# Taking the second router's logits from the weights: `Ws` beside the gate weights, `wo @ Ws` beside `wo`, no transposes of the normalised rows

## The chip, the core and the metric

The kernel runs on one core of a Trainium2 chip. The time is the device time of one execution in microseconds. Five engines matter: TensorE (PE, with its weight loads shown as PEld), VectorE (DVE), ScalarE (ACT), GpSimd (POOL) and SyncE (SP, which here only issues transfers).

## The reference: what is computed

One transformer-like layer on x of shape (8, 512, 256): 4,096 rows of 256, in 32 tiles of 128 rows (four to a batch).

```python
x = x + attention(layernorm(x), ...)      # mixture of 4 memories, gated linear attention,
                                          # ends in: o * rsqrt(mean(o*o)+eps) * norm_w * silu(x@w_g), then @ w_o
x = x + ffn(layernorm(x), Ws, bs, W1, b1, W2, b2)

def ffn(x, ...):                          # N = 4096 rows, E = 8 experts, k = N / E = 512
    route_prob = softmax(xf @ Ws + bs).T
    route_vals, routes = top_k(route_prob, k)
    xin = xf[routes]
    h = gelu(einsum('ekd,edf->ekf', xin, W1) + b1)
    out = (einsum('ekf,efd->ekd', h, W2) + b2) * route_vals
    # added back to the rows that were picked
```

The logits that matter here are `layernorm(x1) @ Ws + bs`, eight numbers a row, where x1 = x + attention output is the residual. A layer norm is (x1 - mean) * rstd, so the same logits are ((x1 @ Ws) - mean * colsum(Ws)) * rstd + bs. And x1 @ Ws is x @ Ws plus (normalised gated rows) @ (w_o @ Ws).

## The kernel before

All instructions are placed by hand on the engines' queues; semaphores order them. The program goes through five stages.

1. **Stage A (0 to 53 us).** For each batch b of 512 rows: DVE takes mean and variance of x and normalises it (`stats_a`, `norm_a`), POOL makes the reciprocal root, PE transposes the normalised rows (`a_transpose`, L1771), ACT copies them out as `xT` (L700), and PE multiplies them by `wgg`, which holds the gate weights w_g (256 columns) and the four columns of the first router, w_gate (`a_product`, L1786, 260 columns, 16 matmul records a batch since each f32 matmul shows as two). ACT makes `gs` (Silu) and `lg` of the result. In the same stage PE turns the low-rank gate weights (`low_rank_t`, before the product of batch 5) and multiplies them out (`merged_gate`, before that of batch 6); ACT copies both (L713, L722), and the next product waits for the first copy. SP issues the loads of x and of the weights and the zero fills of the scatter rooms (`clear_rooms`), one behind the other.
2. **The slots (53 to 463 us).** 24 slots, one attention group of 512 rows each. In slot s PE does, in this order: values, gate of s+1, `outputs(s-1)`, keys, queries, then the items of the output projection, keys turned, values, rows of s+2 turned, `scores(s)`, `updates(s)`. From slot 12 on the output projection and second norm of batch b are spread over the slots: `turned(b)` in slot 12+2b (PE transposes, L1990), `project(b)` in slot 13+2b (@ wo, 256 columns, 16 records), `residual(b)` right behind on DVE (L1271), row statistics on DVE in slot 14+2b (L1279, L1282) with the reciprocal root on ACT, `norm2(b)` on ACT in slot 15+2b (L824, four tiles of rows to `xn2`), `norm_t(b)` on PE in the same slot (eight transposes, L2014) with two ACT copies (L835), and `route(b)` in slot 16+2b (8 narrow matmuls against `wsb` = Ws, 16 records, attn<-wsb), whose result DVE takes to `l8` with the bias added (`router`, L1291). The items sit between fixed PE items of the slot; `scores(s)` waits for them since they share PSUM banks 0 to 3 (`attn`).
3. **The tail (443 to 487 us).** Batches 5, 6 and 7 come out behind the last slot. `outputs(22)` in slot 23 gives the last stored group; SP stores it, POOL gathers batch 7's eight pieces (L467), DVE combines them in two halves (L1302, L1307), then squares, head norm, gate, transposes, projection, residual (`residual_half`, L1333), statistics and second norm in halves, `norm_t_half`, `route_half`, the last logits, a softmax over the eight experts (L1457 to L1467), and the probabilities `p8` are turned on PE.
4. **The search (487 to 533 us).** 15 rounds of DVE, ACT (Sign, L956, after a table load L952) and PE find the 512 best rows of each expert; then the row lists are built.
5. **The experts (533 to 760 us).** Gathers, two products with W1 and W2 for eight experts, scatter with add.

Three orders around the change. SP's queue in the tail is `load_xr(6)`, `store_out(5)`, `store_xp(5)`, `load_xr(7)`, then the stores of 6 and 7. `store_xp(b)` (L642) waits for `norm2(b)`. The residual rows of batches b and b-2 share one buffer, so `load_xr(b)` (L632) waits until `norm2(b-2)` has read it:

```python
if b >= 2:
    sp.wait_ge(out_st[b % 2], 16 * (b // 2))
    sp.wait_ge(f_xn2, TB * (b - 1))
```

ACT's queue behind the last slot begins with `norm2(5)`. And behind the softmax it copies `b1c` (L950) and loads the table for Gelu and Sign (L952) while DVE finishes `p8`.

## Time and profile before

| | us |
|---|---|
| median of 3 runs | 802.74 |
| lowest and highest run | 800.09, 805.4 |
| span of the profiled execution, first to last instruction | 760.2 |
| PE busy | 695.7 (92% of the span) |
| PEld busy | 618.6 (81%) |
| DVE busy | 501.5 (66%) |
| ACT busy | 348.2 (46%) |
| POOL busy | 247.4 (33%) |

The profile gives the profiled execution by its span; the runs' time also holds what lies before the first and behind the last instruction, 42.5 us if the median is set against that span. Times in the trace are microseconds from the start of the span. The chain of work is followed back from the last instruction, at each step to what released it.

### The profile page before, as it was taken

The page shows a single profiled execution, that of the slowest core. Times are in us where ns is not written, and L with a number is a line of the kernel's source. Part 1 is how long each engine was busy: PE and PEld are TensorE (multiplying, and loading weights), DVE is VectorE, ACT ScalarE, POOL GpSimd, SP SyncE. Part 2 cuts the span into 40 slices and gives each one's busy share as a digit, 9 for nine tenths or more (in the row PEclk, how much of TensorE's full clock was granted, in tenths as well). Part 3 has the DMA queues.
Part 4 walks back from the last instruction along what each step waited for, and adds up shares of the span by engine and source line. Part 5 has one row for each costly group of instructions (what it writes and reads, how often), then busy time and mean ns, then how long its engine had stood idle before and what let it go on. Part 6 is the DMA issues. An engine that isn't in the chain of part 4 may idle for free.

```text
span 760.2 us, 25608 instructions
## 1 busy us (share of the span) xinstructions
PE 695.7 (92%) x11058; PEld 618.6 (81%) x11058; DVE 501.5 (66%) x1159; ACT 348.2 (46%) x765; POOL 247.4 (33%) x358
## 2 busy tenths in 40 slices
PE   7998998999989999999999999508999999999993
PEld 6886787989978999899899888407689998999992
DVE  6716774555446678777767677678378878877820
ACT  2663544445544546655656564530353345325410
POOL 5510044555644413223140431001734253203333
PEclk9998999999999999999999998755899999999997
DMA  7960024343443635454544453720735255312213
GB/s 201 391 276 2 31 99 153 109 135 124 157 149 112 196 96 158 135 165 140 168 109 142 138 164 108 262 49 3 233 130 154 54 156 139 120 21 28 29 21 36
DMA packets 75467, 96.81 MB, mean 127 GB/s; under 512 B 11337, under 2 KB 67057, under 8 KB 74202
## 3 DMA queue, kind: packets, MB, share of 16 engines
q1 hardware_dynamic: 62250, 69.52, 28.0%
q0 software_dynamic: 12288, 25.12, 13.2%
q8 instruction: 87, 1.43, 0.8%
q10 hardware_dynamic: 816, 0.53, 0.2%
q14 instruction: 26, 0.21, 0.1%
HBM read 53.78 MB, written 41.55 MB: 125 GB/s over the span
## 4 chain that ended last, share of the span: by engine, by line
PE 78%; DVE 10%; issue 4%; DMA 3%; POOL 2%; ACT 1%; POOLq 0%; DVEq 0%
PE bank L1828 41%; PE attn L1828 27%; PE bank L1786 3%; PE bank L1880 2%; DVE arena L1488 2%; PE bank L1887 1%; DMA arena<-x_p,idxs 1%; PE attn L2189 1%; DMA big<-o_m,gidx 1%; DVE st L1043 1%; PE attn L1771 1%; PE attn L1990 1%; POOL arena L524 1%; POOL big L467 1%; DVE big L1056 1%
## 5 line engine op out<-in xcount | busy, mean ns | idle before, releaser
L1828 PE MATMUL attn<-arena 32*32 32x64 f32 (+4 forms) x6048 | 140.3, 225 | 9.2 <-issue 7.3
L1828 PE MATMUL bank<-xT,arena 128*128 128x128 f32 (+2 forms) x964 | 145.8, 306 | 0.0
L1828 PEld LDWEIGHTS attn<-arena 32*32 32x32 f32 (+3 forms) x6048 | 114.2, 120 | 33.2 <-issue 15.4
L1828 PEld LDWEIGHTS bank<-xT,arena 128*128 128x128 f32 x964 | 124.3, 192 | 11.2 <-issue 5.8
L467 POOL DMA_INDIRECT big<-o_m,gidx x64 | 71.0, 1109 | 159.7 <-PE bank L1828 116.9
L460 POOL DMA_INDIRECT x_c<-big,sidx x64 | 68.6, 1071 | 119.3 <-PE bank L1828 88.9
L1828 PE MATMUL bank<-arena,xT 128*128 128x128 f32 (+2 forms) x640 | 107.1, 320 | 0.1
L1828 PEld LDWEIGHTS bank<-arena,xT 128*128 128x128 f32 x640 | 90.0, 199 | 8.6 <-issue 2.9
L543 POOL DMA_INDIRECT out_dram<-arena,idxs x32 | 50.2, 1569 | 109.6 <-ACT arena L1010 99.3
L1165 DVE COPY_PREDICATED arena<-causal,attn 128x1024 f32<-128x1024 int32 x24 | 31.6, 1316 | 71.2 <-PE attn L1828 71.2
L524 POOL DMA_INDIRECT arena<-x_p,idxs x32 | 34.3, 1070 | 98.8 <-DVE idxs L1567 70.8
L751 ACT ACTIVATE arena<-bank 128x512 f32<-128x512 f32 x48 | 28.7, 599 | 72.1 <-PE bank L1828 72.1
L1828 PE MATMUL bank<-zeros,arena 128*128 128x128 f32 x336 | 39.8, 275 | 0.0
L980 ACT ACTIVATE rmask<-attn 128x512 f32<-128x512 f32 x14 | 8.4, 597 | 67.8 <-PE attn L1828 67.4
L1828 PEld LDWEIGHTS bank<-zeros,arena 128*128 128x128 f32 x336 | 38.7, 192 | 0.1
L965 ACT ACTIVATE big<-big,b1c 128x256 f32<-128x256 f32 x84 | 37.3, 502 | 0.0
L758 ACT ACTIVATE arena<-arena 128x512 f32<-128x512 f32 x24 | 15.2, 633 | 41.9 <-DVE arena L1156 30.3
L1186 DVE SCALAR_TENSOR_TENSOR arena<-arena,bank 128x64 f32<-128x64 f32 x112 | 31.5, 282 | 4.0
L1786 PE MATMUL bank<-wgg,xT 128*128 128x260 f32 x128 | 29.6, 384 | 1.9 <-issue 1.5
L1199 DVE TENSOR_TENSOR_SCAN arena<-rmask,arena 128x512 f32<-128x512 f32 x24 | 29.4, 1226 | 0.8
L1786 PEld LDWEIGHTS bank<-wgg,xT 128*128 128x128 f32 x128 | 23.7, 190 | 5.6 <-issue 2.3
L772 ACT ACTIVATE arena<-attn 64x512 f32<-64x512 f32 x46 | 27.6, 601 | 0.6
(305 smaller groups left out, 1249.2 us busy)
## 6 DMA issues: line engine op xcount, KB each, us to landing
x_c<-zeros SPq DMA_DIRECT2D x8, 1024.0 KB, 9.2
xT<-x_c SPq DMA_DIRECT2D x16, 512.0 KB, 4.1
o_m<-arena SPq DMA_DIRECT2D x16, 512.0 KB, 4.0
xT<-in_L_ffn_W_dram SPq DMA_DIRECT2D x8, 1024.0 KB, 7.9
gs<-in_L_ffn_W_dram SPq DMA_DIRECT2D x8, 1024.0 KB, 7.6
xT<-in_L_attn_x_dram SPq DMA_DIRECT2D x8, 512.0 KB, 5.2
out_dram<-xT SPq DMA_DIRECT2D x8, 512.0 KB, 5.2
arena<-in_L_attn_x_dram SPq DMA_DIRECT2D x7, 512.0 KB, 6.2
```

Source lines behind the costliest of these rows:

```text
L460: nc.gpsimd.indirect_dma_start(x_c[b], bass.IndirectOffsetOnAxis(sidx[:, k, t:t + 1], 0), xn[:, t, :], None, bounds_check=MROWS - 1, oob_i ...
L467: nc.gpsimd.indirect_dma_start(og[:, b % 2, k, j, :], None, o_m[b], bass.IndirectOffsetOnAxis(gidx[:, k, t:t + 1], 0), bounds_check=MROWS ...
L524: nc.gpsimd.indirect_dma_start(xe[:, e % 3, j, :], None, x_p, bass.IndirectOffsetOnAxis(idxs[:, e, j:j + 1], 0), bounds_check=B * S - 1, o ...
L543: nc.gpsimd.indirect_dma_start(outf, bass.IndirectOffsetOnAxis(idxs[:, e, j:j + 1], 0), ye[:, e % 2, j, :], None, bounds_check=B * S - 1, ...
L751: nc.scalar.activation(vv[:, g % 2, 2 * h:2 * h + 2, :], bank[7].rearrange("p (j d) -> p j d", j=2), ACT.Copy).then_inc(d_vs, 1)
L772: ins = nc.scalar.activation(rows[CH * c:CH * c + CH, 2:4, :, :], heads[half(c, 2), 2:4, :, :], ACT.Copy)
L965: nc.scalar.activation(ht[:, f // FT % 2, f % FT, at], ht[:, f // FT % 2, f % FT, at], ACT.Gelu_apprx_tanh, bias=b1c[:, f:f + 1]).then_inc ...
L1165: nc.vector.copy_predicated(am[:, :, :, :], causal[:, :].bitcast(I32).unsqueeze(1).unsqueeze(1).to_broadcast([P, NH, TB, CH]), attn[:, :, ...
L1186: chained(nc.vector.scalar_tensor_tensor(vst[:, c, :], vst[:, c - 1, :], fe[:, g % 2, c - 1:c], u, ALU.mult, ALU.add))
L1199: nc.vector.tensor_tensor_scan(cum[:, :], rmask[:, :], ybuf[:, :], 0.0, ALU.mult, ALU.add)\
L1786: ins = nc.tensor.matmul(bank[4 + j][:, 0:D + M], xT[:, b, k, P * j:P * j + P], wgg[:, k, :], start=(k == 0), stop=(k == 1))
L1828: return nc.tensor.matmul(out_, l, r, start=a, stop=z, skip_group_check=True)
```

## The change

Ws becomes eight more columns of `wgg`, so `a_product` gives x_norm @ Ws beside the gate (268 columns), and `lg` grows to 12 columns. `wo` is scaled by norm_w already in stage A (its two loads move ahead of most weight loads on SP; the scaling moves from slot 7), turned by four more PE transposes in `low_rank_t`, copied by ACT (`wot`), and multiplied by Ws in `merged_gate` (four matmuls, and two more against ones that give the column sums of Ws), so that `wo` has eight more columns, wo @ Ws. Two small ACT copies take these out. POOL turns x_norm @ Ws back to x @ Ws for all rows (`xs`, four operations behind stage A). `project` writes 264 columns into four banks instead of 256 into half banks; `residual` adds `xs` and the eight columns into `l8` with one more DVE operation. `norm_t` and `route`, their ACT copies and the DVE operation `router` are gone, in the slots and in the tail. In their place DVE finishes the logits by four dependent operations (`centred`, `logits`): once for 24 tiles at the end of slot 23, once for batch 6, once for each half of batch 7. The statistics of all batches are kept. In the tail `norm2(5)` moves on ACT from the start of the queue to behind the head norm of batch 7's halves; `norm2_half(1)` moves behind the exponentials, and its shift on DVE behind `p8`; 56 and 24 dummy matmuls (`warm`) stand where 32 and 8 stood.

```diff
-        flat = [ctx.enter_context(nc.psum_tensor(f"bank{i}", [P, 512], F32)) for i in range(4, 8)]
-        bank = [attn[:, i, :] for i in range(4)] + [t[:, :] for t in flat]
+        upper_banks = ctx.enter_context(nc.psum_tensor("bank", [P, 4, 512], F32))
+        bank = [attn[:, i, :] for i in range(4)] + [upper_banks[:, i, :] for i in range(4)]
...
-        wgg = sb("wgg", [P, 2, D + M])
-        wo = sb("wo", [P, 2, D])
+        wgg = sb("wgg", [P, 2, D + M + E])
+        wo = sb("wo", [P, 2, D + E])
...
+            pool.wait_ge(a_lg, NT)
+            pool.wait_ge(w_z, W_Z)
+            nc.gpsimd.tensor_tensor(stda[:, :], vare[:, :, :].rearrange("p b j -> p (b j)"),
+                                    rstda[:, :, :].rearrange("p b j -> p (b j)"), ALU.mult).then_inc(x_s, 1)
+            nc.gpsimd.tensor_tensor(xs_m[:, :, :], means.to_broadcast([P, NT, E]),
+                                    negsum[:, :].unsqueeze(1).to_broadcast([P, NT, E]), ALU.mult).then_inc(x_s, 1)
+            pool.wait_ge(x_s, 1)
+            nc.gpsimd.tensor_tensor(xs[:, :, :], lg[:, :, M:M + E], over_experts(stda[:, :]), ALU.mult).then_inc(x_s, 1)
+            pool.wait_ge(x_s, 3)
+            nc.gpsimd.tensor_tensor(xs[:, :, :], xs[:, :, :], xs_m[:, :, :], ALU.subtract).then_inc(x_s, 1)
...
+            sp.dma_start(wo[:, :, 0:D], kp(w_o)).then_inc(wo_in, 16)
+            for h in range(2):
+                sp.dma_start(nwc[HDV * h:HDV * h + HDV, :], norm_w.rearrange("(n a) -> n a", a=1)).then_inc(wo_in, 16)
...
             clear_rooms(4, B)
-            sp.dma_start(wo[:, :, :], kp(w_o)).then_inc(w_in2, 16)
-            for h in range(2):
-                sp.dma_start(nwc[HDV * h:HDV * h + HDV, :], norm_w.rearrange("(n a) -> n a", a=1)).then_inc(w_in2, 16)
-            sp.dma_start(wsb[:, :, :], kp(Ws)).then_inc(w_in2, 16)
...
+            act.dma_start(wgg[:, :, D + M:D + M + E], kp(Ws)).then_inc(wg_in, 16)
...
+                nc.scalar.activation(wot[:, :, :], upper_banks[:, 2:4, D:2 * D], ACT.Copy)
...
-            norm2(LAST - 2)
             out_t(LAST - 1, (4, 7))
             group_out_last()
             squares_half(0)
-            norm_t(LAST - 2)
             squares_half(1)
             head_rstd_half(0)
             head_rstd_half(1)
+            norm2(LAST - 2)
             out_t_half(0)
             out_t_half(1)
             row_rstd(LAST - 1)
             norm2(LAST - 1)
             row_rstd_half(0)
             norm2_half(0)
-            norm_t(LAST - 1)
             row_rstd_half(1)
-            norm2_half(1)
-            norm_t_half(0)
-            norm_t_half(1)
             for k, (lo, hi) in enumerate(PARTS):
                 act.wait_ge(s_sub, k + 1)
                 nc.scalar.activation(pr[:, lo:hi, :], l8[:, lo:hi, :], ACT.Exp).then_inc(s_exp, 1)
-
+            norm2_half(1)
 
             act.wait_ge(b1_t, 1)
...
+            dve.wait_ge(wo_in, 16 * 3)
+            nc.vector.tensor_scalar(wo[:, :, 0:D], wo[:, :, 0:D], nwc[:, 0:1], None, ALU.mult).then_inc(wo_n, 1)
...
+                nc.vector.tensor_tensor(l8[:, t, :], rows[:, :, D:D + E], xs[:, t, :], ALU.add).then_inc(f_l, 1)
 
...
-            def router(b):
-                dve.wait_ge(f_l, b + 1)
...
+            def lstep(ins):
+                l8_done[0] += 1
+                ins.then_inc(f_l8, 1)
+                dve.wait_ge(f_l8, l8_done[0])
...
+            def centred(lo, hi, from_):
+                n, at = hi - lo, slice(lo, hi)
+                dve.wait_ge(f_mv, hi)
+                dve.wait_ge(f_l, from_)
+                lstep(nc.vector.tensor_tensor(lm[:, at, :], mv[:, at, 0:1].to_broadcast([P, n, E]),
+                                              negsum[:, :].unsqueeze(1).to_broadcast([P, n, E]), ALU.mult))
+                lstep(nc.vector.tensor_tensor(l8[:, at, :], l8[:, at, :], lm[:, at, :], ALU.add))
+
+            def logits(lo, hi, from_):
+                n, at = hi - lo, slice(lo, hi)
+                dve.wait_ge(f_rstd, from_)
+                lstep(nc.vector.tensor_tensor(l8[:, at, :], l8[:, at, :],
+                                              rstd[:, at].unsqueeze(2).to_broadcast([P, n, E]), ALU.mult))
+                lstep(nc.vector.tensor_tensor(l8[:, at, :], l8[:, at, :],
+                                              bsb[:, :].unsqueeze(1).to_broadcast([P, n, E]), ALU.add))
 
...
-                    router(logit)
                 if stats is not None:
                     row_stats(stats)
                 if s == NG - 1:
                     row_stats(LAST - 2)
                     head_scaled(LAST - 1)
                     norm_shift(LAST - 2)
+                if s == NG - 1:
+                    dve.wait_ge(w_in2, 16 * W_IN2)
+                    centred(0, TB * (LAST - 1), LAST - 1)
+                    logits(0, TB * (LAST - 1), LAST - 1)
                 if s >= 1:
                     masked(s)
 
             gated(LAST - 1)
-            router(LAST - 3)
             states(NG - 1)
             combine_half(0)
             combine_half(1)
...
+            centred(TB * (LAST - 1), TB * LAST, LAST)
             norm_shift(LAST - 1)
+            logits(TB * (LAST - 1), TB * LAST, LAST)
             residual_half(0)
             row_stats_half(0)
             residual_half(1)
             norm_shift_half(0)
             row_stats_half(1)
-            norm_shift_half(1)
-            router(LAST - 1)
-            router_half(0)
+            centred(TB * LAST, NT - 2, LAST + 1)
+            logits(TB * LAST, NT - 2, LAST + 1)
 
 
...
+            norm_shift_half(1)
 
 
...
-                        ins = nc.tensor.matmul(bank[4 + j][:, 0:D + M], xT[:, b, k, P * j:P * j + P], wgg[:, k, :],
+                        ins = nc.tensor.matmul(bank[4 + j][:, 0:D + M + E], xT[:, b, k, P * j:P * j + P], wgg[:, k, :],
...
+                pe.wait_ge(wo_n, 1)
+                for k in range(2):
+                    for i in range(2):
+                        nc.tensor.transpose(bank[6 + k][:, D + P * i:D + P * i + P], wo[:, i, P * k:P * k + P],
+                                            ident[:, :])
...
+                pe.wait_ge(c_step, ONES_STEPS)
+                for i in range(2):
+                    for k in range(2):
+                        nc.tensor.matmul(bank[6][:, D + E * i:D + E * i + E], wot[:, k, P * i:P * i + P],
+                                         wgg[:, k, D + M:D + M + E], start=(k == 0), stop=(k == 1))
+                for k in range(2):
+                    ins = nc.tensor.matmul(bank[7][:, 0:E], ones[:, :], wgg[:, k, D + M:D + M + E],
+                                           start=(k == 0), stop=(k == 1))
                 ins.then_inc(w_mm, 1)
 
...
             a_product(0, 0, 2)
...
+                turn, out_ = (step_of(g, f) for f in (12, 13))
                 if turn is not None:
                     pe.wait_ge(f_ont, 2 * turn + 2)
                 if out_ is not None:
                     pe.wait_ge(f_x1, 2 * out_ + 2)
-                if route is not None:
-                    pe.wait_ge(f_xt2, 2 * route + 2)
-                if logit is not None:
-                    pe.wait_ge(f_l8, logit + 1)
+                    pe.wait_ge(f_l, out_ + 1)
                 for j, h, c, lo in product(range(TB), range(NH), range(2), range(2)):
...
-                        ins = mm(bank[at + j // 2][:, D * (j % 2):D * (j % 2) + D], ont[:, k, P * j:P * j + P],
-                                 wo[:, k, :], k == 0, k == 1)
+                        ins = mm(bank[at + j][:, 0:D + E], ont[:, k, P * j:P * j + P], wo[:, k, :], k == 0, k == 1)
...
-            def norm_t(b):
...
-                        ins = nc.tensor.transpose(bank[2 + k][:, P * j:P * j + P], xn2_of[b][:, j, P * k:P * k + P],
-                                                  ident[:, :])
-                    ins.then_inc(f_tp2, 1)
...
-            def route(b, at=2):
...
-                        ins = mm(bank[at][:, E * j:E * j + E], xn2t[:, k, P * j:P * j + P], wsb[:, k, :],
-                                 k == 0, k == 1)
-                ins.then_inc(f_l, 1)
...
                     mm(at[:, 0:P], same_b[:, :], same_b[:, :])
 
-            pe.wait_ge(f_l8, LAST - 2)
             turned(LAST - 1, (4, 7))
             outputs_last()
-            project(LAST - 1, 5)
+            project(LAST - 1, 4)
             pe.wait_ge(d_ob, NG + 1)
-            norm_t(LAST - 2)
-            warm(32, bank[1])
-            route(LAST - 2, 4)
+            warm(56, bank[1])
             turned_half(0)
             turned_half(1)
             project_half(0)
             project_half(1)
-            norm_t(LAST - 1)
-            norm_t_half(0)
-            warm(8, bank[7])
-            route(LAST - 1, 4)
-            norm_t_half(1)
-            route_half(0)
-            route_half(1)
-
-
-            pe.wait_ge(f_l8, B + 1)
+            warm(24, bank[1])
+
+
+            pe.wait_ge(f_l, LAST + 2)
```

## Rows read from the trace of the kernel before

**Rows 1.** The page: the chain that ended last, by engine.
```profile
PE 78%; DVE 10%; issue 4%; DMA 3%; POOL 2%; ACT 1%; POOLq 0%; DVEq 0%
```

**Rows 2.** By stretch: PE, PEld, DVE, ACT, POOL busy; clock; DMA share; GB/s.
```profile
330.00:443.00 113.00, 111.89 (x2541) 100.87 (x2526) 82.01 (x179) 64.72 (x134) 27.08 (x24) 1.00 0.43 133
...
470.00:474.00 4.00, 3.12 (x13) 2.45 (x14) 3.85 (x13) 1.31 (x4) 0.00 (x0) 0.59 0.36 121
```

**Rows 3.** The chain in stage A: start, us, what.
```profile
27.60 3.51 PE bank L1786 x16
...
37.61 0.72 issue
```

**Rows 4.** The chain from batch 7's last gather through the tail into the search.
```profile
457.79 5.99 DMA big<-o_m,gidx
...
475.61 0.70 DVE xT L1333
...
485.15 0.17 DVE l L1458
...
489.44 0.18 PE attn L1828
```

**Rows 5.** The chain in slots 16 and 17.
```profile
324.97 1.69 PE attn L1828 x16
...
341.25 3.45 PE attn L1828 x16
344.70 0.87 PE attn L2014 x8
```

**Rows 6.** Slots 16 and 17 in time: last gather, masks, combine, residual.
```profile
327.28 1.00 POOL L467 DMA_INDIRECT big<-o_m,gidx  x1 [0.30 <-issue]
...
330.81 1.32 DVE L1165 COPY_PREDICATED arena<-causal,attn 128x1024 f32<-128x1024 int32 x1 [2.20 <-PE attn L1828]
...
336.45 1.67 DVE L1241 SCALAR_TENSOR_TENSOR big<-big,wt,zeros 128x256 f32<-128x256 f32 x4
...
344.52 1.28 DVE L1271 TENSOR_TENSOR xT<-attn,xT 128x512 f32<-128x512 f32 x2
```

**Rows 7.** Stage A in time: the last x load on SP, two ACT copies.
```profile
21.05 0.37 SPq L554 DMA_DIRECT2D arena<-in_L_attn_x_dram  x1
...
31.58 1.08 ACT L700 ACTIVATE xT<-attn 128x512 f32<-128x512 f32 x2
```

**Rows 8.** DMA issues by tile: count, KB each, us from issue to landing.
```profile
wo<-in_L_attn_w_o_dram SPq DMA_DIRECT2D x1, 256.0 KB, 10.6
...
nwc<-in_L_attn_norm_w_dram SPq DMA_DIRECT2D x2, 0.2 KB, 9.3
```

**Rows 9.** POOL's groups: busy us, mean ns of one, idle before.
```profile
L392 POOL TENSOR_TENSOR rstda<-vare,negh 128x4 f32<-128x4 f32 x8 | 9.1, 1132 | 14.0 <-DVE vare L1051 10.9 <-issue 1.3 <-POOL causal L380 0.9
...
L433 POOL COPY below<-same 128x128 f32<-128x128 f32 x1 | 0.3, 289 | 0.7 <-DVE same_b L1073 0.7
```

**Rows 10.** DVE in the tail: the second half's last statistics, and `p8`.
```profile
478.94 0.25 DVE L1343 BATCH_NORM_AGGREGATE mv<-st 128x2 f32<-128x6 f32 x2
...
486.30 0.42 DVE L1467 TENSOR_TENSOR arena<-arena,rs 128x256 f32<-128x256 f32 x1
```

**Rows 11.** ACT in the tail: `norm2(5)`, end of batch 7's head norm, table load.
```profile
454.04 2.08 ACT L824 ACTIVATE xT<-xT,shift,rstd 128x256 f32<-128x256 f32 x4
...
469.87 0.21 ACT L869 ACTIVATE hr<-hl 128x8 f32<-128x8 f32 x1
...
485.71 1.28 ACT L952 ACT_TABLE_LOAD   x1
```

**Rows 12.** SP's queue at the end of slot 21: `store_xp(3)`, `load_xr(5)`.
```profile
414.31 0.36 SPq L642 DMA_DIRECT2D x_p<-xT  x1
414.77 0.45 SPq L632 DMA_DIRECT2D xT<-in_L_attn_x_dram  x1
```

**Rows 13.** L632, all eight residual loads, from issue to landing.
```profile
DMA to landing us min/median/max: 4.7/5.2/7.4
```

More of the change, by code:

```diff
@@ L1893, in scores @@
                     pe.wait_ge(d_ob, g)
-                turn, out_, route, logit = (step_of(g, f) for f in (12, 13, 15, 16))
+                turn, out_ = (step_of(g, f) for f in (12, 13))
                 if turn is not None:
@@ L2310 @@
 CONST_STEPS = 26
+ONES_STEPS = 6
+W_Z = 3
 FIRST_STEPS = 2
@@ L2313 @@
 W_TURN = 4
-W_IN2 = 7
+W_IN2 = 3
 W_IN = 1 + 2 * NS
```

177 lines of the change are left out of this document (68 added, 109 removed).

## The prediction, made blind

> **What bounds the kernel now.** I read the chain of waits first: PE holds 78% of the path that ended last [rows 1]. The next view is busy time by stretch. In the slots from 330 to 443 us PE is busy 111.89 of 113 us at the full clock (the column reads 1.00, the level of 2.4 GHz), DVE 82, ACT 65 [rows 2]. So up to `outputs(22)` at 441 us whatever PE no longer does comes off one for one, if nothing it covered shows up. Stage A is also a PE chain from 18 us on: batch after batch of 3.51 us of product and the transposes [rows 3]. In the tail the path is another: batch 7's last gather lands (457.79 + 5.99 us), then DVE, PE and ACT work in turn up to the first count of the search at 489.44 [rows 4]. There PE's items count only where one of the others waits for them. From the search on nothing is edited.
>
> **Slots, what goes.** `route` is 16 records for 1.69 us, `norm_t` eight transposes for 0.87 us [rows 5]. Ahead of `outputs(22)`, behind which batch 7's gathers start, stand `norm_t` of batches 0 to 3 (slots 15, 17, 19, 21) and `route` of batches 0 to 3 (slots 16 to 22): 4 x 0.87 + 4 x 1.69 = 10.24 us. The items of batches 4 and 5 stand behind it, where PE isn't on the path; they count nothing.
>
> **Slots, what is added.** A product of 260 columns takes 3.51 us for 16 records [rows 3], one of 256 takes 3.45 [rows 5]: 0.06 us for 4 columns, so 0.12 us for 8. Five `project` (batches 0 to 4) are on the path: 0.60 us. The new DVE operation in `residual` lies behind the two of L1271, which end at 345.8 [rows 6]; it is about 0.2 us (a 16-element operation takes 0.17 [rows 4]; `router`, which it replaces, was of the same kind). `scores` waits for it, but PE still turns the keys and makes half the values between `project` and `scores`; without that cover it would cost 0.2 us a batch. The other DVE work is equal or less (the scaling of `wo` leaves slot 7). Slots: -9.64 us.
>
> **Stage A.** Six of the eight products are on the chain (batches 2 to 7): 6 x 0.12 = 0.72 us. Four more transposes at 0.87 / 8 = 0.11: 0.44 us. The copy `wot` (128x512) stands on ACT ahead of the copy for which PE already stands idle 0.72 us [rows 3], so it is all on the path; two such copies take 1.08 us [rows 7], one 0.54. In `merged_gate` six narrow matmuls are 12 records at 1.69 / 16 = 0.106 us [rows 5]: 1.27 us. Two tiny ACT copies ahead of the one PE waits for: about 0.1 us each, between nothing, were they hidden, and 0.2 each: 0.20 us. Sum: +3.17 us. The new wait for `wo_n`: the loads of `wo` and `norm_w` follow x load 7, issued at 21.05 [rows 7]. With about 1 us for each issue, the last one starts near 23.7; a landing of 9.3 to 10.6 us [rows 8] gives 33 to 34.3 and with the scaling 34.8 at most. PE comes to the wait near 37.2, just ahead of the stall at 37.61 [rows 3]. It costs nothing, with 2.4 us to spare. The other weight loads on SP move back by these three issues, some 3 us; PE needs them only behind the last product, at 53 us.
>
> **POOL's four operations.** They run behind stage A, while POOL waits for the first lists anyway. What they can do is slow DVE, which is on the path then. No row shows that. The nearest rows are 1.13 us for POOL's two-operand form and 0.29 us for a 128x128 copy [rows 9]: four operations are 1.2 to 4.5 us, of which DVE may lose nothing or about 2. I take +0.5. The Trainium skill ("SBUF — State Buffer", section "SBUF: two separate sides") says that a DVE operation with two SBUF inputs and a GpSimd one that reads SBUF lock each other out for a whole instruction; by it the term would be at the upper end, 2 us, and the sum 798.3. No row here settles it.
>
> **Tail.** Here gains and losses must be laid along the path.
> The gathers start as before behind `outputs(22)`, so the start of `combine_half` at 463.86 is kept relative to it. (DVE's four new operations over 24 tiles in slot 23 are 0.4 us each by the nearest row, `p8` over 32 tiles with 0.42 [rows 10]. They stand ahead of the masks of slot 23 and can push them by up to 1.6 us; PE loses three items of batch 4 and 5 there, 2.56 us and more, and the gathers' transfer is what ends that stretch, so I count nothing.)
> `norm2(5)` stood at 454.04; now it follows batch 7's head norm, which ended at 469.87 + 0.21 = 470.08 [rows 11], plus 0.2 for the DVE operation of `residual(6)`. It takes 2.08 us: 472.36. Only then may SP store its rows and issue `load_xr(7)`, whose buffer it has just read. The load follows the store by 0.46 us [rows 12]: 472.82. Landing takes 4.7 to 7.4 us, median 5.2 [rows 13]; the queues are empty here, so 4.8: 477.6. But `residual_half(0)` started at 475.61 [rows 4]. **It now waits 2.05 us longer, for a transfer instead of for PE.**
> From there to the end of the statistics it was 479.19 - 475.61 = 3.58 us [rows 4, 10]; with two more additions of about 0.18: 481.6. Then four dependent small steps at 0.2 (0.17 [rows 4] and the gap), maximum and subtraction over 30 tiles (0.42 each, as `p8` [rows 10]), four steps for the last two tiles, their maximum and subtraction at 0.2, then two sums, the reciprocal and `p8` (two of them over all tiles at 0.42, two small at 0.25): 0.8 + 0.85 + 0.8 + 0.4 + 1.35 gives 485.8, against 486.30 + 0.42 = 486.72 [rows 10]. The second norm's way through ACT, PE and ACT, which stood here before, saves more than the late load takes: -0.9 us.
> But the first Sign needs its table. Before, ACT loaded it at 485.71 [rows 11], beside the sums. Now ACT first waits for the shift behind `p8` (0.2), does `norm2_half(1)` (half of 2.08, 1.05), copies `b1c` (0.2) and loads (1.28): 485.8 + 2.75 = 488.6, then Sign 0.7 us: 489.3. The count at 489.44 [rows 4] needs both Sign and DVE's comparison. So it stays there: **tail 0**, between +3 (a landing of 7.4) and -2.
>
> **Sum.** +3.17 + 0.50 - 9.64 + 0 = -5.97 us. Against the profiled execution that is a span of 754.2 after 760.2. What lies around the span (42.5 us to the median) is not touched, so the median of 802.74 becomes 796.8 us, 0.74% less.
>
> **Rivals.**
> *A. The tail gains too.* The load lands sooner or the gathers do, since `store_xp(5)` and `load_xr(7)` no longer run beside them (5.99 us for the last [rows 4], with DVE waiting for it). `combine_half` also needs ACT's copies of the last output, which bounds that gain. A landing of 3.2 us would start `residual_half(0)` at 476.1, 1.6 us sooner, and let the table load be the last wait. With nothing lost to POOL: -3.0 us more, 794.0. Against it: none of eight loads landed under 4.7 [rows 13]. The Trainium skill ("DMA: Bandwidth & Descriptors", section "Anatomy of one DMA — SWDGE (gpsimd) path") fits 2.0 us plus bytes over 436e3 per us, for these 512 KB 3.2 us; that is for transfers issued from GpSimd, and the rows here, all from SP, are 1.5 us above it. 0.25.
> *B. The slots give a part back.* What was removed was cover. The last gather of a batch ended its issue at 328.28, and the combine that needs it began at 336.45 [rows 6]. If such a gather needs 5.99 us as in the tail [rows 4], it lands at 334.3; the slot is now 1.69 shorter and the combine comes at 334.8. So 0.5 us are left; with a landing 1 us longer DVE waits 0.5 us a batch, and whatever the removed 2.56 a pair of slots hid beside that (DVE idled 2.20 before its masks [rows 6], which speaks against it) could appear. Half of one route a batch, 4 x 0.85 = 3.4 us: 800.2. 0.22.
> *C. Slower: the wait for `wo_n`.* The rows of `norm_w` are 4 bytes, behind zero fills and x loads. Each microsecond that they land later than 36.7 stalls PE in stage A, and all behind it. From a landing at 42.7 on (19 us after its issue, twice the longest of [rows 8]) the whole gain is gone; at 46 the time would be 806. 0.03.
> *D. The forecast,* 0.46, its own range 795.0 to 798.6.
> *E. The clock.* PE now stands idle some 2 us before batch 7's halves are turned. From 470 to 474 us it was busy 3.12 of 4 us before, and the column already fell to 0.59 there [rows 2]. At the lower level (1.2 GHz) the 16 records of `project_half` would take twice the 3.45 us of [rows 5]; the first half hides behind the late load, the second costs up to 1 us: 797.8. 0.04, inside the forecast's range.
>
> The range: 793.0 to 801.0 us; it takes in most of A and B and POOL's 2 us. A measurement of this kernel can tell about 1% from no change. That is 794.7 and 810.8: faster is most of A and a little of D, 0.27; within 1% the rest of A, D, E and B, 0.70; slower C's end, 0.03.
>
> **What would show it.** In the slots: from slot 15 on a pair of slots is 1.69 + 0.87 - 0.12 = 2.4 us shorter, and PE has no new idle time. Stage A: slot 0 begins 3.2 us later, and the idle time before the product of batch 5 grows from 0.72 to 1.3. Tail: DVE L1333's successor waits for the DMA of `xT<-in_L_attn_x_dram`, about 2 us; `norm2(5)` directly behind the head norm; the table load ends behind DVE's first comparison. Wrong would be: a wait for `wo_n`, gathers that end DVE's idle time in the slots, a residual that still waits for PE, or slots that shrink by less than 2.4 us a pair.

## The result and the profile after

The changed kernel took 813.40 us (median of 4 runs, 808.66 to 817.01) beside 802.65 us of the kernel before (4 runs, 800.09 to 805.40): a ratio of 1.011, 95% interval 1.006 to 1.015. The forecast was 796.8 us; it was wrong, in size and in direction.

The chips differ, which the profiled execution of before hid. Each run now comes with its span, and a run's time is always 1.7 or 1.8 us more than its span. The span of 760.2 us, with its 42.5 us "around it", fits no run of 802 us; it fits a quicker chip. On such a chip (called the quick chip below) the kernel before takes 764.6 us with a span of 762.7; on the four others that ran, and on that of the first comparison, 799 to 803.5. The ratio is nearly the same on both kinds, and times are set only against those of the same chip below; a few readings compare traces across the slower chips and say so. One run of `cheap_best` below was a slow one, 1351.99 us, and is left out of its median.

On the quick chip the kernel before (`before_again`) has a span of 762.7 us, the changed kernel (`after_again`) 775.0. Cut at the masks of DVE (`COPY_PREDICATED`, one per slot) and at the first count of the search:

| stretch | before | changed | difference | forecast |
|---|---|---|---|---|
| start to mask 0 | 67.9 | 72.5 | +4.6 | +3.7 |
| mask 0 to 15 | 247.8 | 243.2 | -4.6 | -0.6 |
| mask 15 to 23 | 141.9 | 152.3 | **+10.4** | **-9.0** |
| mask 23 to first count | 34.6 | 33.1 | -1.5 | 0 |
| first count to end | 270.5 | 274.0 | +3.5 | 0 |

The forecast's -9.64 us is split by where its items stand: `norm_t(0)` and two of the five `project` lie ahead of mask 15. From here on a slot is named by the mask that it begins with: "slot 15" runs from mask 15 to mask 16, and holds most of what the description of the kernel calls slot 16, `route(0)` and `scores(16)` among it.

The slots where PE's items were removed are where the time came from. (Between masks 0 and 15 the changed kernel gained 4.0 us more than forecast; PE was busy 233.2 us there after 237.4, and the granted clock read 0.99 after 0.97.) What PE waited for from mask 15 to 23 in `before_again` (engine, line, releaser: us, times, longest):

```profile
PE attn L1828 <- DVE arena L1190: 1.1, 1, 1.1
```

and in `after_again`:

```profile
PE bank L1862 <- issue: 6.7, 3, 3.1
PE attn L1862 <- issue: 4.4, 2, 2.7
```

"Issue" is a wait for nothing that the profile shows. And the same stretch by busy time (columns as in [rows 2]), `before_again`:

```profile
315.73:457.59 141.86, 140.72 (x3035) 126.56 (x3036) 102.39 (x225) 82.50 (x169) 41.39 (x38) 1.00 0.47 147
```

`after_again`:

```profile
315.69:467.96 152.27, 140.78 (x2992) 122.92 (x2992) 103.87 (x229) 76.69 (x158) 41.65 (x38) 0.93 0.43 137
```

PE was idle 1.1 us of the stretch before, 11.5 now. And it was busy just as long, 140.8 us, with some 9.8 us less to do (four `norm_t` and four `route` less four times 0.12): the granted clock fell from 1.00 to 0.93 of its 2.4 GHz. So the 19 to 20 us between forecast and result in this stretch are about 10 us of gaps and about 10 us of work at the lower clock. One such gap stands in slot 15. The chain there in `before_again` (start, us, what):

```profile
331.03 0.44 PE bank L1880 x4
331.47 1.39 PE attn L1828 x49
332.86 0.59 PE bank L1880 x4
```

The chain in `after_again`:

```profile
330.00 0.94 PE attn L1862 x29
330.94 2.72 issue
333.66 0.34 PE attn L1862 x10
```

The stretches of `after_again` around it:

```profile
330.00:332.00 2.00, 0.94 (x79) 0.77 (x77) 0.00 (x0) 1.61 (x5) 0.33 (x1) 1.00 0.63 213
332.00:334.00 2.00, 0.34 (x18) 0.26 (x19) 0.00 (x0) 0.00 (x0) 0.00 (x0) 1.00 0.04 8
334.00:336.00 2.00, 2.00 (x53) 1.66 (x54) 1.64 (x3) 0.99 (x3) 0.00 (x0) 0.62 0.15 24
336.00:338.00 2.00, 2.00 (x6) 1.55 (x6) 1.82 (x6) 0.00 (x0) 0.00 (x0) 0.53 0.82 262
```

PE stops in the middle of a burst of 32x32 matmuls (`scores`) for 2.72 us, with no wait that the profile shows; then the clock stands at 0.62 and 0.53 for 4 us, near the lower level of 1.2 GHz, and returns.

**Where in the stream the gaps stand.** The page of the profile lists how PE's instructions arrive (queue, kind: packets, MB, share of the 16 DMA engines):

```profile
q8 instruction: 86, 1.41, 0.8%
```

That is 16,384 bytes a packet. I counted every PE record of the trace (matmuls, weight loads, waits) up to each gap:

| gap ends at | us | instructions before it, from the first gap | the 256 before it ran in |
|---|---|---|---|
| 94.03 | 2.11 | 0 | 1.64 us |
| 111.70 | 1.16 | 3 x 256 | 2.18 |
| 156.90 | 0.58 | 12 x 256 | 2.84 |
| 172.71 | 0.88 | 15 x 256 | 2.50 |
| 188.69 | 1.26 | 18 x 256 | 2.42 |
| 333.65 | 2.72 | 44 x 256 | 3.31 |
| 370.62 | 1.64 | 50 x 256 | 2.40 |
| 409.53 | 2.58 | 56 x 256 | 2.23 |
| 429.48 | 1.08 | 59 x 256 | 1.66 |
| 449.31 | 3.06 | 62 x 256 | 1.91 |

All of them, the ten over 0.5 us, stand at multiples of 256 (to one record), and so do those of the kernel before on this chip (131.53 and 229.89 us, 2.2 and 2.8 us, are the large ones). Between 90 and 470 us no gap of PE over 0.35 us put down to issue stands elsewhere in these two traces. And counted from the first PE record, these gaps of both kernels and of `norm2_back`, all on this chip, end at the 194th or 195th record of a group of 256, though the kernels have different instructions there; those of `before_shift` below, whose stream is moved by 128, at the 193rd to 195th. The trace has 22,075 PE records, the queue 86 packets: 257 records a packet. 256 instructions are called a page below.

PE's next packet starts 1.1 to 1.3 us after the end of seven of the ten gaps (1.7 to 2.2 after the other three) and takes 0.9 to 1.4 us; matmuls go on 1.2 to 1.6 us after the end of the last packet. From entering one page to running the next it took 2.7 to 6.0 us at these gaps, 3.7 in the middle. The reading that fits: PE asks for a page about when it enters the one before, and can run it some 3.6 us later, later still when the packet is late (at 333.65 it had started 3.6 us after PE entered the page before). That data transfers delay it there is not shown. A page of 128x128 matmuls lasts longer: 16 records take 1.79 us (slot 15), so a page of 128 with their weight loads some 14, an estimate. One that lies wholly in the bursts (176 matmul records in 2.2 us, each with its weight load) does not. The Trainium skill says the same of the structure ("Advanced Engine Details and Errata", section "ISA Cache": two lines of 16 KB, 256 instructions each) but counts the crossing as "mostly hidden" ("Runtime: NRT & Kernel Launch", section "Instruction fetch mechanics"). The first agrees with the 256 of this trace; by the gaps above the second does not hold for bursts of small matmuls.

### The profile page after: what moved, and what is told of

The parts are those of the page before. It is cut to its first block, busy times and chain, and to the rows that moved or that the text cites. A ratio compares the mean times of both kernels' runs of the same rounds, so it can differ in the third digit from the quotient of the medians.

```text
span 806.9 us, 25331 instructions
## 1 busy us (share of the span) xinstructions
PE 701.5 (87%) x10922; PEld 612.8 (76%) x10922; DVE 508.2 (63%) x1175; ACT 341.4 (42%) x752; POOL 245.0 (30%) x362
## 4 chain that ended last, share of the span: by engine, by line
PE 78%; DVE 9%; issue 7%; ACT 3%; DMA 1%; another core or an unknown queue 1%; POOL 1%; SPq 0%; ACTq 0%; DVEq 0%; POOLq 0%
PE bank L1862 41%; PE attn L1862 27%; PE bank L1807 3%; PE bank L1914 2%; DVE arena L1509 2%; PE bank L1921 1%; PE attn L2165 1%; DVE st L1049 1%; PE attn L1792 1%; PE attn L2021 1%; DMA xT<-in_L_attn_x_dram 1%; DVE gs L1574 1%; DVE big L1062 1%; DMA arena<-in_L_attn_x_dram 0%
## 5 line engine op out<-in xcount | busy, mean ns | idle before, releaser
L1862 PE MATMUL attn<-arena 32*32 32x32 f32 (+4 forms) x6048 | 152.9, 227 | 28.1 <-issue 26.8
L1862 PEld LDWEIGHTS attn<-arena 32*32 32x32 f32 (+3 forms) x6048 | 121.1, 121 | 58.0 <-issue 44.2
L483 POOL DMA_INDIRECT big<-o_m,gidx x64 | 66.7, 1041 | 180.5 <-PE bank L1862 129.0
L1862 PE MATMUL bank<-arena,xT 128*128 128x128 f32 (+2 forms) x640 | 109.3, 322 | 3.1 <-issue 3.1
L770 ACT ACTIVATE arena<-bank 128x512 f32<-128x512 f32 x48 | 28.7, 597 | 94.3 <-PE bank L1862 72.3
L1807 PE MATMUL bank<-wgg,xT 128*128 128x268 f32 x128 | 32.8, 413 | 2.6 <-issue 2.1
L1194 DVE SCALAR_TENSOR_TENSOR arena<-arena,bank 128x64 f32<-128x64 f32 x112 | 31.6, 282 | 4.0
L1862 PE MATMUL attn<-arena,xT 128*128 128x256 f32 (+1 forms) x96 | 27.0, 422 | 5.2 <-DVE idxs L1588 5.2
L799 ACT ACTIVATE arena<-bank 128x512 f32<-128x512 f32 x24 | 14.4, 599 | 37.1 <-PE bank L1921 33.8
```

The source lines that it names most:

```text
L483: nc.gpsimd.indirect_dma_start(og[:, b % 2, k, j, :], None, o_m[b], bass.IndirectOffsetOnAxis(gidx[:, k, t:t + 1], 0), bounds_check=MROWS ...
L770: nc.scalar.activation(vv[:, g % 2, 2 * h:2 * h + 2, :], bank[7].rearrange("p (j d) -> p j d", j=2), ACT.Copy).then_inc(d_vs, 1)
L1194: chained(nc.vector.scalar_tensor_tensor(vst[:, c, :], vst[:, c - 1, :], fe[:, g % 2, c - 1:c], u, ALU.mult, ALU.add))
L1807: ins = nc.tensor.matmul(bank[4 + j][:, 0:D + M + E], xT[:, b, k, P * j:P * j + P], wgg[:, k, :], start=(k == 0), stop=(k == 1))
L1862: return nc.tensor.matmul(out_, l, r, start=a, stop=z, skip_group_check=True)
```

## The experiments

**Controls: both kernels unchanged, and the tail.** `norm2_back` undoes one move of the change:

```diff
+            norm2(LAST - 2)
             out_t(LAST - 1, (4, 7))
...
-            norm2(LAST - 2)
             out_t_half(0)
```

> The kernel before, unchanged, for its spans. In the changed kernel's trace PE stands idle some 40 us in gaps of 0.4 to 2.6 us that are put down to issue, nearly all ahead of the 32x32 matmuls; in the trace of the kernel before, such gaps add up to about 12 us, and its span of 760.2 us lies 42.5 us under the median of its runs, where the changed kernel's lies 1.8 us under. Theory 'typical': the timed runs of the kernel before have such gaps too, and its profiled execution was a rare quick one. Then this trace shows a span of 797 to 804 us with 1.8 us around it, and 30 us or more of PE idle time put down to issue. Rival 'made by the change': a span near 760 with about 42 us around it, and some 12 us of such gaps.

> The changed kernel, unchanged, on the same chip as the kernel before. If the gaps of PE belong to the kernel, the ratio is 1.010 again and the gaps stand in the same slots as in the first trace of it (486 to 494 us, slots of batch pairs). If they come by chance, the time stays within 805 to 820 but the gaps move, and the ratio may be anything from 1.00 to 1.02.

> The changed kernel with norm2(5) directly behind the slot loop again on ACT, as before the change. Theory 'late load': in the changed kernel residual_half(0) waits 2.8 us for the load of x, issued only when norm2(5) had read the buffer. Here the load lands early, DVE does not wait for it, the last residual starts about 2.8 us sooner, and the table load of ACT becomes what the first count waits for as far as DVE's chain now ends sooner: the whole is 1.5 to 2.8 us shorter than the changed kernel (-0.2 to -0.35%). Rival 'cover': norm2(5) now delays out_t(6), the squares and the head norm of batch 7 by up to 2.1 us, and nothing is won (0 to +1 us).

One chip, before 764.63 us (22 runs). `before_again`: 764.58, ratio 1.000 [0.997, 1.002]; page gaps up to 490 us add up to 8.1 us. So "typical" was wrong for this chip, and "made by the change" wrong about the 42 us: it was the chip. `after_again`: 774.55, 1.013 [1.010, 1.016], page gaps 17.7 us. `norm2_back`: 771.25, 1.010 [1.007, 1.013], 3.3 us less, with intervals that overlap; its gaps in slots 15, 17, 20, 21 and 22 stand at the same counts as those of `after_again` (1.6, 1.3, 2.5, 0.8, 3.0 us): they belong to the kernel. Its tail, mask 23 to first count, is 31.6 us against 33.1, and its way from the first count to the end 270.3 against 274.0. That last is not the instruction stream. PE's longest wait there in `after_again` is in the experts, at 559, where nothing was edited:

```profile
PE attn L2165 <- DMA arena<-x_p,idxs: 2.8, 1, 2.8
```

It waits for a gather to land, as DVE does at the same moment; `before_again` waits 1.2 us there, `norm2_back` not at all. Behind it, from 559 to 570 us, the clock read 0.85, after 1.00 in `before_again`.

**The place in the stream.** Tiny matmuls (32x32, unused) at 7 us, where PE waits for the first batch: 32 of them (`before_shift`) are 128 instructions (two matmul records and two weight loads each), 64 (`before_page`) are 256, and 56 in the changed kernel (`after_shift`) are 224.

```diff
             a_warm(13)
+            tiny(bank[7], 32)
             a_first()
```

> The kernel before with 32 tiny matmuls (32x32) more on PE at 7 us, where PE waits for the first batch anyway: nothing else is changed, and only the place of every later PE instruction in its stream moves, by 128 instructions. In the traces every gap of PE put down to issue stands at a multiple of 256 instructions (16 KB, the size of one instruction packet), and a gap comes where the 256 instructions before it ran in less than about 3.6 us (1.2 us to the packet's start, 1.1 us of packet, 1.3 us to the next matmul). Theory 'pages': by the times of the kernel before, this shift puts a page's end behind each burst of small matmuls in 22 slots: 36 us of gaps at 3.6 us a fetch (56 at 4.5) instead of 3 (14), and the clock falls behind the gaps: 35 to 70 us slower, about 800 to 835. Rival 'missing cover': the gaps of the changed kernel come because the removed matmuls no longer give the fetch time, and the place in the stream does not matter: within 1 us of the kernel before.

> The changed kernel with 56 tiny matmuls (224 instructions) at the same early place. With the 32 instructions that the change adds in stage A this is a whole page, so up to slot 15 every instruction lies in its page as in the kernel before. Theory 'pages': the gaps of slots 1 to 9 go, those from slot 15 on stay (13 us instead of 18 in the changed kernel by the same reckoning): 3 to 7 us less than the changed kernel, 768 to 772. Rival 'missing cover': no less than the changed kernel, 774 to 776.

> The control for before_shift: 64 tiny matmuls instead of 32 at the same place, 256 instructions, so that every later instruction is moved by one whole page and lies in its page as before. Theory 'pages': within 2 us of the kernel before (the tiny matmuls run while PE waits for the first batch). Rival 'the added matmuls cost': as much as before_shift or more, 1.02 and up.

`before_shift`: 819.90 us beside 799.18, **1.025 [1.021, 1.030]**: half a page of shift alone costs 20.7 us. `before_page`, twice as many added instructions: 805.56 beside 803.53, 1.002 [0.999, 1.004], nothing. Between masks 15 and 22 `before_shift` takes 138.4 us and has 8 page gaps, `before_page` 128.1 and none (two of the slower chips; the trace of `before_shift` is of its longest run, 825.32 us). PE's waits from mask 15 to 22 in `before_shift`:

```profile
PE bank L1834 <- issue: 6.6, 7, 1.3
PE attn L1834 <- issue: 2.2, 5, 0.7
```

and in `before_page`:

```profile
PE attn L1834 <- issue: 1.9, 6, 0.4
```

That settles the cause against "missing cover" as the whole of it, since here nothing was removed. The size was off: 20.7 us, not 35 to 70. The reckoning came from the quick chip; on the slower chips the bursts run slower by themselves (below), which gives a page more time: redone on the trace of `before_third` it gives 28 us of gaps in place of 35, and the trace of `before_shift` has 17. By the same reckoning the kernel before happens to stand at nearly the best of all 256 places of its stream (3 us of gaps at 3.6 us a fetch, 35 at the worst). `after_shift`, which repairs the place only up to slot 15: 806.78 beside 799.18, 1.011 [1.007, 1.015], no better than the changed kernel's 1.011 and 1.013; the forecast of 3 to 7 us less failed within what the intervals can tell, and its trace still has 8.2 us of page gaps.

**Padding.** Where the change took instructions out, the same number is put back as tiny matmuls, ahead of `keys_t`:

```diff
             def keys_t(g):
                 pe.wait_ge(d_kd, g + 1)
+                tiny(bank[5], 4 * (step_of(g, 15) is not None) + 8 * (step_of(g, 16) is not None))
```

> As after_shift, and in slots 15 to 23 as many instructions are put back as the change took out, ahead of keys_t: 4 tiny matmuls for norm_t, 8 for route (0.05 to 0.1 us a slot instead of 0.87 and 1.69). Theory 'pages': nearly all gaps go (3 us left, as before), the clock stays up, and what was forecast for the slots comes out: 15 to 18 us less than the changed kernel, 757 to 760 us, that is 0.990 to 0.995 of the kernel before. Rival 'missing cover': PE gets no more time per page than in the changed kernel, so the gaps of slots 15 to 23 stay and the time is 773 to 776.

> As after_padded, with norm2(5) directly behind the slot loop again. norm2_back was 3.3 us less than the changed kernel (intervals overlap). Theory 'late load': 2 to 3 us less than after_padded, 754 to 758 us. Rival: the difference of norm2_back was chance, and this equals after_padded within 1 us.

> The kernel before, unchanged, for a trace on the same chip as the next three. If this is a chip on which it takes some 800 us, the trace should show where the 36 us against the quick chip go: both theories of the change expect them to be the same for every kernel (the traces of the other kernels on such chips have some 35 gaps of 0.4 to 0.6 us in the bursts of small matmuls, away from the page ends, 15 to 20 us together). On a quick chip: a span of 758 to 766.

> after_padded once more, for its trace beside the kernel before on the same chip. On a quick chip: 757 to 761 us, 0.990 to 0.996. On a slow one: 0.995 to 1.000 as measured, and against before_third the trace shows where the rest of the forecast 6 us went: stage A (+4 to +5, with the clock lower over the last two products), slots 15 to 22 (-7 to -9), tail (-1.5).

`after_padded`: 798.26 beside 799.18, 0.998 [0.995, 1.001], against 1.011 unpadded; page gaps up to 490 us are 2.6 us, against 11.7 in the changed kernel's first trace (a slower chip too). The forecast of 15 to 18 us less was for the quick chip, where no padded kernel ran; in ratios, the pages give back 1.3% of the 1.8% between forecast (0.993) and result (1.011). `padded_back` (with `norm2` moved back as above): 793.45, 0.994 [0.991, 0.996], 4.8 us less than `after_padded`, of which the traces show 2.5 in the tail. `padded_again` on another chip: 802.93 beside 803.53, 0.999 [0.997, 1.001]. Against `before_third` (804.19, same chip) the stretches differ from what was expected. To mask 0 it is 5.4 us longer (expected 4 to 5). From mask 15 to 22 it takes 126.5 us after 128.5, 2.0 less and not 7 to 9. From mask 23 to the first count it takes 33.3 after 39.0, 5.7 less and not 1.5 (`before_page` takes 39.0 too); the clock there read 0.76 after 0.72, which can't be all of it, and the rest stays open. So on the slower chips the tail holds most of what the change gains. Part of what is missing in the slots are the pads, here in the timeline of `padded_again` (start, us, engine, line, operation):

```profile
406.75 0.43 PE L1784 MATMUL bank<-ident 32*32 32x32 f32 x8
```

0.37 us for 8 records up to the next item, where 0.05 to 0.1 us was expected; all stand on the same 32 rows. Twice that where `route` was: 4.4 us over the slots.

**Cheaper pads, full pads.** `cheap_pads` lets the tiny matmuls go round the four groups of rows (8 records then take 0.20 us); `full_pads`, built on it, gives PE its time back, with the sizes of the removed work but from constants, its output unused:

```diff
+                for _ in range(8 * (step_of(g, 15) is not None)):
+                    nc.tensor.transpose(bank[5][:, 0:P], ident[:, :], ident[:, :])
+                for _ in range(8 * (step_of(g, 16) is not None)):
+                    mm(bank[5][:, 0:E], ident[:, :], ident[:, 0:E])
```

> As after_padded, but the tiny matmuls go round the four groups of 32 rows instead of standing all on one. In padded_again 8 records of them took 0.43 us, so the pads cost 0.37 us in a norm_t slot and twice that in a route slot, 4.4 us over slots 15 to 22; the small matmuls of scores, which alternate between groups, take 11 ns a record. Theory 'forecast holds for the slots at a fixed place in the pages': 3 to 4 us less than after_padded, 0.990 to 0.995 of the kernel before. Rival: the pads were hidden and nothing changes (0.998).

> As cheap_pads, with matmuls of the removed sizes instead of tiny ones, from constants and unused: 8 transposes 128x128 for norm_t, 8 matmuls of 8 columns for route, the same count of instructions at the same place. This gives PE's time back and nothing else of the removed work. The forecast's largest term, 4 x (0.87 + 1.69) = 10.24 us less the cheap pads (4 x 0.3), says: 8 to 10 us more than cheap_pads. Rival 'cover': the time was needed (the gaps inside the bursts or ACT's copies of the turned rows take its place): 3 to 6 us more.

One chip, before 803.41: `cheap_pads` 800.88, 0.996 [0.994, 0.998]; `full_pads` 804.27, 1.001 [0.999, 1.003]. **PE's removed time is worth 3.4 us here (about 2 either way by the two intervals), not 8 to 10**: with the instruction stream held equal, the largest term of the sum gives more than half back. The stretch from mask 15 to 22 (columns as in [rows 2]), `cheap_pads`, then `full_pads`:

```profile
336.94:463.71 126.77, 120.60 (x2691) 105.17 (x2696) 89.22 (x192) 68.45 (x140) 33.54 (x32) 1.00 0.45 143
337.24:465.86 128.62, 126.55 (x2692) 113.31 (x2696) 89.13 (x192) 68.57 (x140) 33.57 (x32) 1.00 0.45 140
```

PE is busy 6.0 us less, and idle 4.1 us more (6.2 after 2.1): the time that PE no longer works is mostly time in which it stands still. The slots that had `norm_t` shrink by 0.6, 0.2 and 0.5 us. Of the `route` slots one shrinks by 0.85 and one by 0.16, one stays (17.54 after 17.56), one is 0.55 longer, because gaps come up. PE's waits from 332 to 462 us in `full_pads`:

```profile
PE attn L1869 <- issue: 1.8, 5, 0.4
```

and in `cheap_pads`:

```profile
PE attn L1869 <- issue: 3.1, 7, 0.9
PE bank L1921 <- issue: 1.3, 2, 0.8
PE bank L1921 <- ACT xT L764: 0.2, 1, 0.2
PE attn L1869 <- ACT big L850: 0.2, 1, 0.2
```

**POOL and the burst.** The slower chips have a second kind of gap, inside pages: in `before_third` 39 over 0.3 us between masks 0 and 23 put down to issue, 20.3 us together, where the quick chip has none. In the traces of slower chips all of those over 0.35 us between 100 and 470 us (25 to 34 a trace) begin while POOL issues an indirect DMA or within 1 us behind it, though that covers only half of the time. With `route` cheap the burst starts sooner and comes closer to POOL's last two gathers, as the timeline of `cheap_pads` in slot 15 shows:

```profile
350.67 1.00 POOL L483 DMA_INDIRECT big<-o_m,gidx  x1 [0.30 <-issue]
351.72 0.49 PE L1921 MATMUL bank<-ident,xT 128*128 128x128 f32 x3
352.71 0.27 PE L1921 MATMUL bank<-ident,xT 128*128 128x128 f32 x1 [0.51 <-issue]
352.91 1.22 PE L1869 MATMUL attn<-arena 32*32 32x64 f32 x103
355.06 0.37 PE L1869 MATMUL attn<-arena 32*32 32x32 f32 x25 [0.93 <-issue]
```

(the second gap, 0.93 us, is a page's end). `held` moves them behind the burst:

```diff
                     gather_back(b, 3, 6)
-                    pool.wait_ge(d_q, s + 1)
+                    pool.wait_ge(d_u, s + 1)
                     gather_back(b, 6, 8)
```

> cheap_pads with POOL's last two gathers of each batch issued behind the burst of small matmuls (they waited for the queries of the slot, now for its updates). On the slower chips 33 of 34 gaps over 0.35 us inside the bursts stand while POOL issues an indirect DMA or within 1 us of one, though POOL does that only 48% of the time; on the quick chip there are none. In cheap_pads these gaps add up to 5.5 us in slots 15, 17, 19 and 21, in full_pads to 1.8: with route gone the burst starts 1.2 us sooner and meets the last two gathers. Theory 'POOL meets the burst': the gaps of these four slots shrink to under 1 us in sum; the time falls by 2 to 4 us if the later gathers still land before DVE combines them (361.1, they would land at 361 to 364), or stays, with DVE waiting for the DMA. Rival 'not POOL': the gaps stay at 5 us.

`held`: 799.41 beside 803.09, 0.996 [0.993, 0.998], the same ratio as `cheap_pads`. Masks 15 to 22 fell to 123.5 us, 3.3 less than `cheap_pads` and 5.0 less than `before_third` (three chips), and the gaps of the four route slots from 5.5 to 2.5 us (not under 1). Slot 10, batch 0's gathers, took it back: 21.7 us after 17.5, with 2.3 us of gaps and the clock at 0.84; right ahead of it stands a page gap of 2.3 us that is 0.5 in `cheap_pads`. So part of those gaps does follow POOL's issues; why PE loses time beside them, and only on some chips, no run here tells.

**The tail, and all together.** `padded_table` and `cheap_best` are `padded_back` and `cheap_pads` with this edit too (`cheap_best` also with `norm2` moved back); `held_best` is `held` with both:

```diff
-            norm2_half(1)
...
             act.preload_act_table_set("gelu_apprx_tanh_and_others")
+            norm2_half(1)
```

> padded_back with norm2_half(1) on ACT behind the load of the table. In norm2_back the first count waited 0.9 us for ACT's Sign, whose table was loaded only after norm2_half(1) (1.09 us), while DVE's comparison had ended. Theory 'table last': 0.9 to 1.1 us less than padded_back. Rival: something else is last and nothing changes (0 to 0.2 us).

> cheap_pads with both edits of the tail: norm2(5) directly behind the slot loop, norm2_half(1) behind the load of the table. By norm2_back (-3.3 us), padded_back (-4.8) and padded_table against padded_back (about -1, across chips not to be told): 4 to 6 us less than cheap_pads, 0.984 to 0.990 of the kernel before. Rival: the tail's gain is used up with the pads gone: 0.990 to 0.995.

> held with both edits of the tail (norm2(5) behind the loop, norm2_half(1) behind the load of the table): 1 to 6 us less than held; 0.985 to 0.995 of the kernel before.

`padded_table`: 799.20 beside 803.53, 0.996 [0.993, 0.999]; mask 23 to first count is 29.9 us after 33.3 in `padded_again`, of the same chip, and 30.9 in `padded_back` of another: both edits together are worth 3.4 us of tail, the table 1.0 of them if chips don't differ here. `cheap_best`: 799.40 beside 803.41, 0.995 [0.993, 0.997], only 1.5 less than `cheap_pads` instead of 4 to 6, which is what its tail gave (31.4 us after 33.0). `held_best`: 797.53 beside 803.09, 0.993 [0.991, 0.996], 1.9 less than `held`, its tail 31.7 after 33.8. So the versions that keep the change, pad it and put one or both of the tail's operations elsewhere (`padded_back`, `padded_table`, `cheap_best`, `held_best`) are 0.4 to 0.7% below the kernel before, the best of them about where the change alone was forecast.

## Why the prediction was wrong, point by point

**"Up to `outputs(22)` whatever PE no longer does comes off one for one, if nothing it covered shows up."** This step failed, in two ways. The first is among no rival. The path was PE's, but PE has an input that I didn't list: its own instructions. Taking out 16 instructions with each `norm_t` and 32 with each `route` moved every later page's end, and from slot 15 on these fell behind the bursts. The term was -9.64 us, of which -9.0 falls between masks 15 and 23; that stretch gave +10.4. Hints stood in the trace on which the prediction rests, two waits "issue" in the chain of earlier slots, which I left aside:

```profile
129.21 2.72 issue
...
223.93 2.90 issue
```

The second way is that even a PE whose stream is in place does not give back "one for one": at a fixed place in the stream 3.4 us are left instead of 8 to 10 on a slower chip, since 4.1 of the 6.0 us that PE was busy less between masks 15 and 22 came back as gaps. Rival B ("the slots give a part back") has this outcome, but mainly by DVE waiting for gathers, and in `cheap_pads` DVE waits for none. In the sums themselves there are only slips of 0.1 us or less (2.05 for 477.6 - 475.61; rival A comes to 793.8 and not 794.0), and rival C's 19 us is twice the 9.3 us of `norm_w` and not twice the longest of [rows 8].

**The time around the span.** I added 42.5 us where 1.8 belong. It did next to no harm to the ratio, but it hid that the trace showed a quicker chip than the one that was timed.

**Clock.** Rival E put its loss in the tail, 1 us at most. It came in the slots, some 10 us, behind all five page gaps from mask 15 on.

**Stage A**, +3.17 forecast, +4.6 measured to mask 0. PE's timeline in `after_again`:

```profile
37.86 0.60 PE L1820 MATMUL bank<-ident,wo 128*128 128x128 f32 x4
38.39 0.22 PE L1822 MATMUL bank<-ident,arena 5*128 5x5 f32 x1
39.81 3.85 PE L1807 MATMUL bank<-wgg,xT 128*128 128x268 f32 x16 [1.20 <-issue]
43.50 1.04 PE L1792 MATMUL attn<-ident,big 128*128 128x128 f32 x8
44.47 2.49 PE L1827 MATMUL bank<-arena 16*128 16x128 f32 x20
46.89 1.11 PE L1832 MATMUL bank<-wgg,arena 128*128 128x8 f32 x8
47.85 1.00 PE L1835 MATMUL bank<-wgg,ones 128*128 128x8 f32 x4
49.73 9.86 PE L1807 MATMUL bank<-wgg,xT 128*128 128x268 f32 x32 [0.88 <-issue]
```

The product takes 3.85 us after 3.75 (forecast 0.12 more), the stall grew from 0.72 to 1.20 (forecast 0.54), the second from 0.73 in `before_again` to 0.88 (forecast 0.20), and nothing waits for `wo_n`: right, term by term. The twelve narrow records took 1.9 us instead of 1.27, and the last two products 9.86 (clock 0.77 from 50 to 60 us) after 8.91 in `before_again`, where 0.24 more was forecast: these two make the rest.

**POOL's operations**: 2.29 us in all, between 60.17 and 62.46. One DVE operation beside them, of 0.29 us before, took 0.73, and slot 0 was as long as before (PE's first matmul of it to mask 0: 13.0 us in both). So the term was 0, not +0.5. The 0.73 us may show the lock that the Trainium skill describes ("SBUF — State Buffer", section "SBUF: two separate sides"), but the operand of that operation is also laid out otherwise now, and nothing was late for it.

**Tail**, forecast 0 (+3 to -2), measured -1.5. Its chain came out step by step: head norm, `norm2(5)`, store, load, then the wait, and at its end ACT's copy and table. The chain in `after_again`:

```profile
482.27 2.07 ACT xT L844 x4
...
484.36 0.36 SPq L657
...
484.82 5.34 DMA xT<-in_L_attn_x_dram
...
497.33 0.42 DVE arena L1487
497.76 0.08 DVE shift L1377
...
497.86 1.09 ACT zeros L898 x2
498.96 0.11 ACT b1c L956
...
499.08 1.28 ACT L958
...
500.38 0.61 ACT arena L962 x2
```

From the load's issue to the end of `p8` it is 12.9 us (forecast 13.0), though the landing was 5.3 us, not 4.8, and from there to the first count 3.3 (forecast 3.6). DVE waited 2.9 us for the load (forecast 2.05). Rival A's short landing did not come: the eight loads took 4.8 to 6.2 us. So the 3.2 us that I worked out, as an estimate, from the Trainium skill ("DMA: Bandwidth & Descriptors", section "Anatomy of one DMA — SWDGE (gpsimd) path") do not carry over to these transfers, which SP issues. In `norm2_back`, without the late load, the tail is 1.5 us shorter. On the slower chips the tail shrank by more than the range allowed (33.3 us after 39.0); the forecast was worked out on the trace of a quick one.

**Search and experts**, forecast 0: +3.5 us on the quick chip in the profiled run, of which 1.6 is a longer wait for a gather of the experts (2.8 after 1.2 us), and most of the rest the lower clock behind it. `norm2_back` has neither (-0.2 us), so this may be chance.

## What to carry to other kernels

PE's instruction stream is a transfer like any other: here 16 KB pages, with about 3.6 us from entering one page to the moment when the next can run. Where a kernel runs bursts of tiny matmuls, count the instructions between them before taking any out: adding 128 moved all later pages, and that alone was worth 2.5% here. This change could be judged fairly only with its stream padded to the old places, and the sign to look for was a wait "issue" in the middle of a burst.

## What the runs showed of the hardware

- A page's end behind a burst stopped PE for 0.4 to 3.1 us. Behind six of the ten gaps of the table (2.11 us, and the five from 333 us on) the clock read 0.50 to 0.69 over the next 4 us, behind the other four (0.58 to 1.26 us) 1.00. From mask 15 to 23 the clock cost about as much as the gaps (10 us each, quick chip).
- The same kernel takes 764.6 us on one chip and 799 to 803.5 on four others. Of the 35 to 39 us between them 20 are gaps inside pages, beside POOL's indirect DMAs; the rest, and why, stays open.
- Tiny matmuls all on the same 32 rows took 46 ns a record, the same ones going round the four groups of rows 25 ns, those of `scores` 11 ns.
